# First head group's maxima moved into the projection stage, with one PSUM tile shared by q and k

## The reference

```python
B, S = x.shape                                   # 2, 2048
h = emb[x]                                       # 256 columns
Q, K, V = (heads(wq, bq), heads(wk, bk), heads(wv, bv))
score = jnp.einsum('bhsd,bhtd->bhst', Q, K) / jnp.sqrt(jnp.float32(D_K))
attn = jax.nn.softmax(score, axis=-1)
o = jnp.einsum('bhst,bhtd->bhsd', attn, V)
```

## Time and profile before

| | us |
|---|---|
| median of three runs | 3424.03 (3408.75 to 3426.32) |
| the profiled execution | 3430.8 |
| its span, first to last instruction | 3429.0 |
| mean granted TensorE clock | 0.968 |
| TensorE busy | 3235.7 (94%) |
| VectorE busy | 2913.3 (85%) |
| ScalarE busy | 2734.0 (80%) |
| GpSimd busy | 1449.0 (42%) |

### The profile page before, as it was taken

The page is one execution under the profiler, slowest core; times in us unless marked ns, Lnnn a source line. Parts: engine busy times, 40 slices in busy tenths (PEclk is TensorE's granted clock), DMA queues, the critical chain, the costliest instruction groups (busy, mean ns, idle before and its releaser), DMA issues. The chain is left out here.

```text
span 3429.0 us, 75632 instructions
## 1 busy us (share of the span) xinstructions
PE 3235.7 (94%) x26913; PEld 2179.4 (64%) x26913; DVE 2913.3 (85%) x2894; ACT 2734.0 (80%) x4665; POOL 1449.0 (42%) x1379
## 2 busy tenths in 40 slices
PE   8599999999999999977899999999999999998898
PEld 7233333333333333336799999999999999986665
DVE  4789999999979999824599999999999999999422
ACT  3078888888878888842799999999999999999344
POOL 3100000000000000000588899998888899899200
PEclk9589999999989999988999999999999999999999
DMA  8420312112020200033111121211111111112431
GB/s 221 86 26 5 43 18 30 24 23 35 11 42 6 38 9 5 5 81 111 39 51 63 63 69 63 69 51 63 63 63 63 66 66 63 57 45 99 143 116 55
DMA packets 94154, 192.81 MB, mean 56 GB/s; under 512 B 16804, under 2 KB 31940, under 8 KB 92296
## 3 DMA queue, kind: packets, MB, share of 16 engines
q1 hardware_dynamic: 82616, 174.28, 18.5%
q10 hardware_dynamic: 9680, 9.84, 0.9%
q0 software_dynamic: 1536, 4.20, 0.8%
HBM read 136.64 MB, written 51.12 MB: 55 GB/s over the span
## 5 line engine op out<-in xcount | busy, mean ns | idle before, releaser
L1258 POOL TENSOR_TENSOR m_g<-m_hs,m_cb 128x512 f32<-128x512 f32 x1024 | 1286.0, 1287 | 175.5 <-PE m_ps_y L1290 89.8
L608 DVE TENSOR_REDUCE a_mx<-a_ps_m 128x2 f32<-128x1024 f32 x1024 | 1241.5, 1223 | 85.9 <-PE a_ps_m L466 68.4
L584 ACT ACTIVATE a_probs<-a_ps_s 128x512 f32<-128x512 f32 x2048 | 1110.5, 596 | 200.1 <-PE a_ps_s L496 156.0
L1390 DVE TENSOR_TENSOR_SCAN m_hs<-m_da,m_carry,m_ps_x 128x512 f32<-128x512 f32 x768 | 930.2, 1263 | 19.8 <-issue 8.0
L466 PE MATMUL a_ps_m<-a_k,a_q 48*128 48x512 f32 x2048 | 774.9, 471 | 35.6 <-DMA a_q<-q_scr 21.2
L496 PE MATMUL a_ps_s<-a_q,a_k 50*128 50x512 f32 x2048 | 774.7, 458 | 7.7 <-ACT a_probs L584 2.9
L1347 ACT ACTIVATE m_da<-m_delta,m_a_cur 128x512 f32<-128x512 f32 x1024 | 715.2, 713 | 0.0
L503 PE MATMUL a_ps_o<-a_probs,a_v 128*32 128x256 f32 x8192 | 669.0, 399 | 8.5 <-ACT a_o L571 8.0
L1278 PE MATMUL m_ps_x<-m_ident,m_bu 128*128 128x128 f32 x4096 | 627.6, 276 | 50.5 <-DVE m_hs L1390 32.1
L1290 PE MATMUL m_ps_y<-m_ident,m_g 128*128 128x128 f32 x4096 | 616.2, 273 | 0.6 <-POOL m_g L1258 0.6
L1332 ACT ACTIVATE m_bu<-m_dut,m_bt 128x512 f32<-128x512 f32 x832 | 593.8, 714 | 15.1 <-PE m_ps_x L1278 14.8
(11 more groups left out here) (150 smaller groups left out, 2525.6 us busy)
## 6 DMA issues: line engine op xcount, KB each, us to landing
m_cb<-c_scr SPq DMA_DIRECT2D x128, 512.0 KB, 3.7
y_scr<-m_ysb SPq DMA_DIRECT2D x16, 1024.0 KB, 6.5
ffn_y<-y_scr SPq DMA_DIRECT2D x14, 1024.0 KB, 7.4
a_k<-k_scr SPq DMA_DIRECT2D x96, 128.0 KB, 6.6
a_q<-q_scr SPq DMA_DIRECT2D x96, 128.0 KB, 8.9
q_scr<-p_partsq SPq DMA_DIRECT2D x16, 512.0 KB, 3.9
k_scr<-p_partsk SPq DMA_DIRECT2D x16, 512.0 KB, 6.3
m_xn<-xn_scr SPq DMA_DIRECT2D x16, 512.0 KB, 5.0
```

The lines of the kernel that those rows point to most:

```text
L584: nc.scalar.activation(probs[:, t % PR, HEADS[j]], turned(i), ACT.Exp, scale=float(DK) ** -0.5).then_inc(exped, 1)
L608: nc.vector.reduce_max(mx[:, i:i + wide], ps_m[:, b:b + wide], AX.X).then_inc(m_maxed, 1)
L1258: nc.gpsimd.tensor_tensor(g[:, t % NG], hs[:, t % NHS], cb[:, quarter % 2, n % CQ], ALU.mult).then_inc(g_ok, 1)
L1390: nc.vector.tensor_tensor_scan(hs[:, t % NHS, rev], da[:, t % NDA, rev], ps_x[:, t % NX, rev], carry[:, n, i:i + 1] if p else 0.0, ALU.mul ...
```

## The change

The 64 max products and 32 reductions of the first head group's first chunk move out of the head of stage 2 into stage 1, among the work of chunks 5, 6 and 7: 10, 11 and 11 pairs of products. For this `a_k`, `a_q`, `a_mx` and `a_neg` are allocated ahead of both stages, the loads of head group 0 are issued by SyncE in chunk 4 (heads 0 and 1 ahead of chunk 4's stores, heads 2 and 3 behind them), and the two memsets of ones open VectorE's program. The pairs need PSUM: they have one tile of two banks (`ps_first`), and to make room q and k share one tile (`ps_qk`). TensorE's order in a chunk becomes q, transposes of the next chunk, v, k, and the projection of q waits until the low part of the last k is made. Both stages now have one set of semaphores, so the clearing and its barrier between them go. `a_neg` is reduced at the end of stage 1; stage 2 opens with its transpose and the ten early pairs.

```diff
+BLK = HG * NC * NC
+FIRST_PAIRS = {NC + 1: (0, 10), NC + 2: (10, 21), NC + 3: (21, BLK // 2)}
...
-        ps_qk = [pb(f"p_ps_{n}", [P, KD, CH], FP32) for n in "qk"]
+        ps_qk = pb("p_ps_qk", [P, KD, CH], FP32)
+        ps_first = pb("p_ps_first", [P, 2, CH], FP32)
...
+                    if n == NC:
+                        for a in range(2):
+                            for half in range(2):
+                                sp.wait_ge(stored[a][half], ONE + 16 * PARTS * NC // 2)
+                        sp.wait_ge(at.ones_first, ONE + 2)
+                        load_heads(sp, at, q_scr, k_scr, 0, 0, range(2))
...
+                    if n == NC:
+                        load_heads(sp, at, q_scr, k_scr, 0, 0, range(2, HG))
...
+                def project(n, a, m):
+
+                    buf = n % 2
+                    if m == 0:
+                        pe.wait_ge(ht_ok, ONE + n + 1)
+                        pe.wait_ge(parts_ok[1 - a], ONE + n + a)
...
+                def first_pair(p):
+
+                    i = 2 * p
+                    if i % 32 == 0:
+                        for half in range(2):
+                            pe.wait_ge(at.loaded[0][2 * (i // 32) + half], ONE + 32 * len(Q_PART))
+                    pe.wait_ge(at.m_maxed, ONE + p)
+                    pair, st, tc = i // 32, i // 8 % 4, i // 2 % 4
+                    for half in range(2):
+                        row = half * (P // 2)
+                        nc.tensor.matmul(ps_first[:, half], at.q_st[row:row + KQ, 0, 0, pair, st * P:(st + 1) * P],
+                                         at.k_st[row:row + KQ, 0, pair, tc * CH:(tc + 1) * CH],
+                                         start=True, stop=True).then_inc(at.m_scored, 1)
...
+                    for m in range(KD):
+                        project(n, 0, m)
+                        some(1)
                     if n + 1 < B * NC:
                         turned(n + 1)
...
+                    some(1)
+                    value_rows(n, (0, 1))
+                    some(1)
+                    value_rows(n, (2, 3))
+                    some(2)
+                    for m in range(KD):
+                        project(n, 1, m)
+                        some(1)
+                    some(BLK)
...
             @block.vector
             def _(dve):
+                for first in (P // 4, 3 * P // 4):
+                    nc.vector.memset(at.k_st[first:first + P // 4, 0].bitcast(FP32), 1.0).then_inc(at.ones_first, 1)
                 dve.wait_ge(ids_in, ONE + 16)
...
+                def first_maxima(p):
+
+                    dve.wait_ge(at.m_scored, ONE + 2 * p + 2)
+                    nc.vector.reduce_max(at.mx[:, 2 * p:2 * p + 2], ps_first[:, :, :], AX.X).then_inc(at.m_maxed, 1)
...
+                    some(1)
+                    low(n, 0)
+                    some(1)
                     if n + 1 < B * NC:
                         turned_low(n + 1)
+                    some(3)
                     dve.wait_ge(v_mm, ONE + n + 1)
...
+                    some(2)
+                    low(n, 1)
+                    some(BLK)
...
-                for item in range(BLK + HG * EARLY):
-                    if item == FIRST_NEG:
-                        transpose_neg(0)
-                    max_blocks(item // BLK, 0, item // BLK, item % BLK, item % BLK + 1, loads if item < BLK else None)
+                transpose_neg(0)
+                max_blocks(1, 0, 1, 0, HG * EARLY, None)
```

More of the change, by code:

```diff
@@ L2 @@
 from concourse import mybir
+from collections import deque
 from contextlib import ExitStack, contextmanager
@@ L72, in identity, with __init__, load_heads, embed_and_project @@
                        pattern=[[-1, tile.shape[1]]], channel_multiplier=1).then_inc(done, 1)
-def embed_and_project(nc, sem, x, emb, weights, biases, q_scr, k_scr, v_all):
+BLK = HG * NC * NC
+FIRST_PAIRS = {NC + 1: (0, 10), NC + 2: (10, 21), NC + 3: (21, BLK // 2)}
+class FirstBlock:
+    def __init__(self, sem, k_st, q_st, mx, neg):
+        self.k_st, self.q_st, self.mx, self.neg = k_st, q_st, mx, neg
+        self.loaded = [[sem(f"loaded{p}{h}") for h in range(HG)] for p in range(2)]
+        self.m_scored, self.m_maxed, self.neg_ok, self.ones_first = sem("m_scored"), sem("m_maxed"), sem("neg_ok"), sem("ones_first")
+def load_heads(sp, at, q_scr, k_scr, g, buf, heads, parts=range(len(Q_PART))):
+    for h in heads:
+        first, pair = h % 2 * (P // 2), h // 2
+        for stack, scr, part in ((at.k_st, k_scr, K_PART), (at.q_st, q_scr, Q_PART)):
+            src = scr.rearrange("a b (g h d) s -> a (b g) h d s", h=HG, d=DK)
+            for i in parts:
+                rows = src[part[i], bass.ds(g, 1), h].rearrange("g d s -> (g d) s")
+                dst = stack[first + i * DK:first + (i + 1) * DK, buf].bitcast(FP32)
+                if stack is at.k_st:
+                    sp.dma_start(dst[:, pair], rows).then_inc(at.loaded[buf][h], 16)
+                else:
+                    sp.dma_start(dst[:, :, pair], rows.rearrange("d (c s) -> d c s", s=CH)).then_inc(at.loaded[buf][h], 16)
+def embed_and_project(nc, sem, at, x, emb, weights, biases, q_scr, k_scr, v_all):
     with ExitStack() as ctx:
@@ L183, in _, with some @@
                 for n in range(B * NC):
[L184 to L191, removed]
+                    pairs = deque(range(*FIRST_PAIRS.get(n, (0, 0))))
+                    def some(count):
+                        for _ in range(min(count, len(pairs))):
+                            first_pair(pairs.popleft())
+                    for m in range(KD):
+                        project(n, 0, m)
+                        some(1)
                     if n + 1 < B * NC:
                         turned(n + 1)
[L194 to L198, removed]
+                    some(1)
[7 more added lines that the diff above has]
+                    some(BLK)
             @block.scalar
@@ L286, in attention @@
         NM = HG * NC
[L287 to L289 removed]
+        mx, neg = at.mx, at.neg
         neg_col = sb("a_neg_col", [NM, P], FP32)
@@ L357, in _, with load @@
             def _(sp):
[L358 to L371 removed]
+                def load(g, buf):
+                    load_heads(sp, at, q_scr, k_scr, g, buf, range(HG))
                 def store_neg(m, buf, c):
@@ L612, in maxima @@
                                          AX.X, negate=True).then_inc(neg_ok, 1)
-                for first in (P // 4, 3 * P // 4):
-                    nc.vector.memset(k_st[first:first + P // 4, 0].bitcast(FP32), 1.0).then_inc(ones_first, 1)
-                with dve.Fori(0, G * NC) as m:
+                with dve.Fori(1, G * NC) as m:
                     maxima(m)
```

97 lines of the change are left out of this document (44 added, 53 removed).

## The result

The changed kernel took 3461.65 us (median of 7 runs, 3446.86 to 3468.84), the kernel before, on the same chip and in the same hours, 3421.06 (3407.39 to 3435.87): a ratio of 1.0127 [1.0106, 1.0148], slower by about 40 us where 21 were forecast. The direction held; the size did not.

A forecast was written before the change was run, and what follows sets the result against it. Stage 1 was taken as bound by TensorE, the head of stage 2 by VectorE. Paying 3.7 + 12.0 + 6.1 + 44.8 + 4 = 70.6 against 49.7 saved gave 20.9 us later: 3445 us, range 3424 to 3462.

The forecast's parts named there:

- three such starts less some cover: 4: Stage 1, chunk starts after the pairs: TensorE starts at 1.2 GHz, costing 4 us, bounds 0 and 11.
- The clock falls all through stage 1: Rival, stage 1: q starts at 1.2 GHz at seven chunk starts, 11 instead of 4; 3452 to 3462, chance 0.15.
- load wait and pairs: Stage 1 from q of chunk 5: waiting for loads adds 6.1 us, the pairs in chunks 5 to 7 add 44.8.
- The price of a start, 1.6: Stage 1: a dense projection starting at 1.2 GHz loses 1.6 us, 10.83 for chunk 0 against 9.27.
- The memsets: Head of VectorE's program: the two memsets delay the first step on token ids by 3.7 us, bounds 0 and 5.
- The shared tile: Starts of chunks 1 to 5: q waits for k's low part, 2.4 us each, 12.0 in all.
- The wait for the loads: Before pair 0 in chunk 5: TensorE waits 6.1 us for the first heads' loads, bounds 1 and 9.
- the estimate from the Trainium skill: Loads before pair 0: about 2.0 us plus bytes at 436 GB/s per transfer, wait nearly nothing, some 6 us less.
- The chain of the pairs at a full clock: Chunks 5 to 7: product, reduction and next product form links of 1.88 us; an eleven-pair chunk takes 24.8.
- The saving: Between the end of stage 1 and the first score: 19.0 us instead of 68.7, so 49.7 saved.
- the limb named: Head of stage 2: GpSimd's queue decides, first score 17.7 us after its first memset, against 16.5 for early reductions.
- The rival in which the pairs hide: Rival, chunks 5 to 7: VectorE's busy time binds, 23 instead of 44.8; 3419 to 3424, chance 0.08.

The follow-up runs named there:

- the seventh run: Changed kernel with unread filler matmuls behind k in every chunk, ahead of pair 0 and behind pairs ending chunks 5 to 7; 3459.79 us, ratio 1.0118.
- the second run: Changed kernel with ten unread matmuls behind k in chunks 0 to 4, filling the stop; 3468.74 us, ratio 1.0166.
- the sixth run: Changed kernel with each product reduced by itself and the tile's two banks used in turn; 3461.62 us, ratio 1.0147.
- the first run: Kernel before with only the tile shared by q and k and the order q, transposes, v, k; 3455.42 us, ratio 1.0115.
- the third: Changed kernel with the two memsets of ones on GpSimd behind its gathers of chunks 2 and 3; 3454.88 us, ratio 1.0104.
- the fifth: Changed kernel without the 64 products and 32 reductions in stage 1, first chunk's maxima zeros; 3423.20 us, ratio 1.0007.
- the ninth run: Kernel before with head group 0's loads in chunks 4 to 7, memsets on GpSimd, no semaphore barrier, stage 1 not awaiting its last stores; 3410.28 us, ratio 0.9999.

## Why the prediction was right in direction and too small in size

**The clock is the step that failed.** The forecast took "three such starts less some cover: 4" for it, and kept "The clock falls all through stage 1" as a rival with a chance of 0.15. That rival is what happened. It priced the clock at 11 and 10, together 21, and its 3452 to 3462 just holds the measured 3461.65. The clock's term is 17 to 18, not 4, and it is made up like this.

At the starts of chunks 1 to 4 it cost 1.56 each, 6.2 in all (13.38 against 11.82 with the stop filled). From q of chunk 5 to the last maximum the stretch took 90.8 instead of the 28.5 + 50.9 = 79.4 of load wait and pairs, 11.4 more; the load wait took 0.5 less, so 11.9 stand beside the pairs. For chunk 6 the seventh run shows that most of this is the clock: 26.4 at 1.00 with the fillers' 1.3 in it, 29.7 at 0.73, so 3.3 measured and 4.5 by the estimate without them. The 0.4 by which that estimate (25.2) lies above the forecast's 24.8 belongs to the chain: pair and half of q take 2.00 (121.65 to 123.65), where 1.70 with the hand-off were taken. For chunks 5 and 7 the clock is argued from rows alone: pairs of 0.80 and halves of q of 2.93 instead of 1.66, with links of 2.13 instead of 1.84.

The argument I held against the rival, that the clock rises again within a chunk and each fall is short, was right for chunks 1 to 4 (the q of each is back at speed before k) and wrong about the sum: a cheap fall came at nearly every stop, and among the pairs the falls were not short (0.73 over chunk 6). The reason I gave for three starts only was that the end of a pair chunk is idle; a stop of 2.31 us behind a chunk of dense matmuls was followed by a fall too. The price of a start, 1.6, held, although its source was weaker than I took it for. I read the slow q of chunk 0 as time at 1.2 GHz, but the granted clock over it in the trace of before reads 1.00, so only its duration spoke for that; the 1.56 of the second run bears the size out.

```profile
19.20:24.00 4.80, 4.80 (x14) 3.85 (x15) 0.00 (x0) 0.24 (x1) 2.22 (x3) 1.00 0.96 94
```

**The memsets** are the second, smaller error: 6.0, outside its bounds of 0 and 5. The term took the engines' start (0.75) from a ScalarE row; VectorE's memset started at 1.66, and the 0.91 between the two memsets, which is lost on this path, was left out. The trace of before has that gap, between the same two memsets in stage 2 (from 103.91 to 104.82).

**What held.** The shared tile: stops of 2.31 with 2.4 forecast, 2.55 a chunk with them filled. The wait for the loads: 5.60, forecast 6.1, where the estimate from the Trainium skill (DMA: Bandwidth & Descriptors, Anatomy of one DMA) gave nearly none; the page's fit is for transfers that GpSimd issues, and these are SyncE's. The chain of the pairs at a full clock: links of 1.84 and a chunk of 25.2 by the estimate above, forecast 1.88 and 24.8. The saving: 50.6, forecast 49.7, on the limb named, GpSimd's memsets and staging, which now stand ahead of the low part at 196.40; the barrier cost 0.3 and not 0.8. The rival in which the pairs hide needed chunk 6 below 18 us, and it took 29.7; even with the banks in turn, in the sixth run, VectorE waits 24.1 us for its products. The Trainium skill (Perfetto Trace Analysis, Optimizing Tensor Performance, Matmuls) named both the tile and the pairs' chain as losses; the first run puts the tile at 28.6 with its clock, so its direction held here.

**The sum again, as measured:** 6.0 + 12.8 (five stops of 2.55) + 6.2 (clock, chunks 1 to 4) + 5.6 + 44.8 + 11.9 - 50.6 = 36.7. The 44.8 is the forecast's and the 11.9 what is left over beside it, so these two are measured only together, as 56.7.

## What to carry to other kernels

Where an engine runs dense work at full clock, price a new stop twice: the stop itself, and the matmuls behind it at 1.2 GHz (here 2.3 us and 1.6 us), at every place where it comes, not once. An estimate that takes a chain of waits at full clock holds only where the clock stays there. Sharing one PSUM tile between two products in a row cost such a stop each time here, and it is worth looking at that edit alone before looking at what it made room for. Work that is moved into a stage to lie beside other work must find not only an idle engine there but a place in the order of both engines, and loads moved with it must find DMA engines that are not full.

## What the hardware showed that was not expected

- Nearly every stop of 2.31 us of TensorE between chunks of dense 512-column matmuls was followed by a fall to the 0.5 level, so that the next twelve took up to 4.58 us instead of 2.96: 4 of 4 such groups in the changed kernel, 6 of 7 in the first run (the last took 3.01), 4 of 4 in the third, 6 of 7 in the fifth (one took 3.00). With the stop filled by matmuls that nobody reads, the granted clock read 1.00 over 47 us. The Trainium skill (TensorE: Matmul & The Clock Gate, A second HAM failure mode: psum-queue depth-cycling) tells of a kernel whose short idle times between groups of matmuls, made by its PSUM buffers, let the clock swing between its two levels; the trace here agrees, 0.87 over chunk 1 and 0.73 over chunk 6.
- In the attention the same 12235 matmuls took from 1307 to 1341 us in single executions, the longer the lower the mean granted clock (0.99 to 0.96).
- With the DMA engines full (share 1.06), SyncE took 3.61 us to issue two stores of 512 KB, and the next stage started only behind it (101.93 and 101.97, in the ninth run).
